# A four-layer model on one core: row statistics taken where the rows are finished, gates multiplied in at the expert slots, GpSimd joining a token's two expert rows, the input loaded in four pieces

## The reference

```python
def _layernorm(x, axis=-1, eps=1e-05):
    m = jnp.mean(x, axis=axis, keepdims=True)
    v = jnp.var(x, axis=axis, keepdims=True)
    return (x - m) / jnp.sqrt(v + eps)

for layer in range(4):
    xn = _layernorm(x)
    x = x + attn[layer](xn) + ffn[layer](xn)
```

```python
g = softmax(xn @ Wr)
top2_w, top2_idx = top_k(g, 2)
top2_w = top2_w / sum(top2_w)                 # layer 2 only
y = relu(xn @ W1[e]) @ W2[e]                  # for every expert e
out = sum(top2_w * y[top2_idx])
```

## Time and profile before

| what | value |
|---|---|
| time, median of 3 runs | 1793.24 us (1793.17 to 1802.02) |
| the profiled execution, its own time | 1782.04 us |
| its span | 1780.2 us |
| PE, PEld | busy 88%, 61% of the span |
| DVE, ACT, POOL | busy 66%, 56%, 21% |
| layer 0's second pair stage | from about 385 to 742 us of the span |
| norm stages of layers 1, 2, 3 | begin at 742.0, 1131.8, 1450.8 us |

### The profile page before, as it was taken

How to read it: one execution, slowest core, us unless ns; L and a number is a source line. 1 busy time by engine, 2 the same in 40 slices (tenths; PEclk the granted TensorE clock), 3 DMA queues, 4 the chain that set the end, 5 groups by cost and what they waited for, 6 DMA issues and landing times. The chain is left out here.

```text
span 1780.2 us, 31999 instructions
## 1 busy us (share of the span) xinstructions
PE 1575.2 (88%) x10960; PEld 1094.2 (61%) x10960; DVE 1183.5 (66%) x3106; ACT 1002.4 (56%) x2683; POOL 375.5 (21%) x386
## 2 busy tenths in 40 slices
PE   4799999959999999899999989588989957899986
PEld 2577777726666666567778766355556733555653
DVE  5599998747777777646545434577743358999964
ACT  2488887706666666444454434133453427888845
POOL 0100000000000000010122015332452410888830
PEclk8899999979999999989999999799999978999998
DMA  4000000040000000110000011400012130233200
GB/s 141 1 1 1 1 1 1 1 141 1 1 1 1 1 1 1 55 57 1 13 16 16 25 31 64 165 1 1 15 36 62 46 90 14 88 86 89 86 21 24
DMA packets 43980, 62.50 MB, mean 35 GB/s; under 512 B 7576, under 2 KB 29920, under 8 KB 43008
## 3 DMA queue, kind: packets, MB, share of 16 engines
q1 hardware_dynamic: 39280, 51.08, 9.6%
q0 software_dynamic: 4544, 9.38, 1.5%
HBM read 49.88 MB, written 15.75 MB: 37 GB/s over the span
## 5 line engine op out<-in xcount | busy, mean ns | idle before, releaser
L591 ACT ACTIVATE probs<-psum_all,pair_negmax 128x256 f32<-128x256 f32 x512 | 235.8, 473 | 158.9 <-DVE pair_negmax L690 86.7
L2116 POOL TENSOR_TENSOR weighted<-state,c_all 128x512 f32<-128x512 f32 x128 | 163.6, 1298 | 77.5 <-DVE state L2126 62.5
L690 DVE TENSOR_REDUCE pair_negmax<-psum_all 128x2 f32<-128x512 f32 x192 | 123.6, 685 | 66.9 <-PE psum_all L506 66.9
L2126 DVE TENSOR_TENSOR_SCAN state<-decay,psum_all 128x512 f32<-128x512 f32 x128 | 148.9, 1199 | 15.4 <-PE psum_all L2044 12.5
L716 DVE TENSOR_SCALAR probs<-probs,pair_recip 128x256 f32<-128x256 f32 x512 | 146.1, 349 | 4.5
L506 PE MATMUL psum_all<-keys,queryT 64*128 64x256 f32 x1024 | 143.9, 400 | 2.8 <-ACT probs L591 2.7
L602 ACT ACTIVATE probsT<-psum_all 128x512 f32<-128x512 f32 x256 | 140.0, 611 | 0.7 <-PE psum_all L517 0.5
L531 PE MATMUL psum_all<-probsT,values 128*64 128x256 f32 x1024 | 138.8, 392 | 0.0
L517 PE MATMUL psum_all<-ident,probs 128*128 128x128 f32 x1024 | 133.1, 273 | 2.8 <-ACT probsT L602 1.9
L517 PEld LDWEIGHTS psum_all<-ident,probs 128*128 128x128 f32 x1024 | 119.1, 141 | 18.1 <-issue 4.4
L506 PEld LDWEIGHTS psum_all<-keys,queryT 64*128 64x128 f32 x1024 | 92.6, 189 | 54.6 <-issue 46.6
(11 more groups left out here) (369 smaller groups left out, 3281.4 us busy)
## 6 DMA issues: line engine op xcount, KB each, us to landing
c_all<-c_rows SPq DMA_DIRECT2D x64, 256.0 KB, 3.3
slots<-slot_fill_dram SPq DMA_DIRECT2D x2, 2535.0 KB, 14.6
ring<-slots SPq DMA_DIRECT2D x18, 260.0 KB, 3.0
keys<-found SPq DMA_DIRECT2D x16, 256.0 KB, 4.7
up<-up_dram SPq DMA_DIRECT2D x1, 2048.0 KB, 7.8
down<-down_dram SPq DMA_DIRECT2D x1, 2048.0 KB, 12.3
up<-up_dram SPq DMA_DIRECT2D x1, 1408.0 KB, 6.1
found<-values,dest POOLq DMA_INDIRECT x78, 2.2
```

What stands on the lines that cost most here:

```text
L591: nc.scalar.activation(k.probs[:, 2 * (u % PAIR_BUF) + j, t, :], k.psum[score_bank(u, j)][:, SEQ * t:SEQ * (t + 1)], ACT.Exp, bias=k.pair_ ...
L690: nc.vector.reduce_max(k.pair_negmax[:, u % 2, SUB * j:SUB * (j + 1)], src, AXX, negate=True).then_inc(s.negmax_ready, 1)
L2116: nc.gpsimd.tensor_tensor(w.weighted[:, u % RING, :], w.state[:, u % RING, :], w.c_all[:, u // L3_DC % C_RING, :], ALU.mult)\
L2126: nc.vector.tensor_tensor_scan(w.state[:, u % RING, :], w.decay[:, u % L3_RING, :, :].rearrange("p b n -> p (b n)"), k.psum[u % PARTS_RING ...
```

## The change

It has six parts.

1. Statistics. A new `measure` issues `bn_stats` for some tiles, waits, and issues `bn_aggr` for them. `add_output` calls it for the two tiles of each sequence, `sparse_experts_stage` for each chunk of four tiles. `layer_norm_stage` then starts from the moments, except in layer 0.
2. The input is loaded by four transfers of 256 KB with a semaphore each, and `measure` runs on each when it has landed. TensorE waits for `ident` alone.
3. Gates travel with the rows: `gate_rows` copies the two gates behind each row, `SLOT_WIDTH` is 132, and layer 2's renormalising moves from step 20 to step 13.
4. In the expert stage three small VectorE instructions per chunk choose each slot's gate, ScalarE multiplies by it while it saves the result, and ScalarE and SyncE wait for the gates.
5. GpSimd adds the two rows of each token, one add of 128x512 for each chunk of four tiles. VectorE adds the sum to `k.x` by one add of 128x512, in place of eight instructions.
6. The expert stage has four more semaphores.

```diff
-SLOT_WIDTH = P + 2
+SLOT_WIDTH = P + 4
...
+def measure(nc, k, dve, step, tiles):
+
+    for t in tiles:
+        step.add(nc.vector.bn_stats(k.stats[:, t, :], k.x[:, t, :]))
+    step.wait()
+    for t in tiles:
+        step.add(nc.vector.bn_aggr(k.moments[:, t, :], k.stats[:, t, :]))
...
                 if first is not None:
-                    sp.dma_start(k.x[:, :, :], first).then_inc(s.x_loaded, 16)
+                    for c in range(CHUNKS):
+                        sp.dma_start(k.x[:, CT * c:CT * (c + 1), :], first[:, CT * c:CT * (c + 1), :]).then_inc(chunk_loaded[c], 16)
                     sp.dma_start(k.ident[:, :], k.dram["ident"]).then_inc(s.x_loaded, 16)
...
                 if first is not None:
-                    dve.wait_ge(s.x_loaded, 32)
-                for t in range(TILES):
-                    step.add(nc.vector.bn_stats(k.stats[:, t, :], k.x[:, t, :]))
-                step.wait()
-                for t in range(TILES):
-                    step.add(nc.vector.bn_aggr(k.moments[:, t, :], k.stats[:, t, :]))
-                step.wait()
+                    for c in range(CHUNKS):
+                        dve.wait_ge(chunk_loaded[c], 16)
+                        measure(nc, k, dve, step, range(CT * c, CT * (c + 1)))
+                    step.wait()
...
                 if first is not None:
-                    pe.wait_ge(s.x_loaded, 32)
+                    pe.wait_ge(s.x_loaded, 16)
                 keep_running(nc, k, 7, 5)
...
                     nc.vector.tensor_tensor(rows, k.mix[:, :, :], yb[:, 0:SEQ].rearrange("p (t n) -> p t n", t=SUB), ALU.add).then_inc(s.output_added, 1)
+                    dve.wait_ge(s.output_added, q + 1)
+                    measure(nc, k, dve, step, range(tile, tile + SUB))
...
+def gate_rows(nc, k, w, dve, s, step):
+
+    step.wait()
+    step.add(nc.vector.tensor_copy(w.rows[:, :, P + 2:P + 4].rearrange("p t r -> p r t"), k.gate_top[:, :, :]))
...
     if g == at.pick:
         gate_pick(nc, k, w, dve, s, step)
-    if g == at.renormalise and renormalise:
-        gate_renormalise(nc, k, w, dve, s, step)
+        if renormalise:
+            gate_renormalise(nc, k, w, dve, s, step)
+        gate_rows(nc, k, w, dve, s, step)
...
                     sp.wait_ge(s.dest_ready, c - CHUNK_RING + 1)
+                    sp.wait_ge(s.slots_gated, c - CHUNK_RING + 1)
...
-                        nc.scalar.activation(w.y_rows[:, j % 4, :], k.psum[6 + j % 2][:, 0:P], ACT.Copy).then_inc(s.y_saved, 1)
+                        act.wait_ge(s.slots_gated, j // SLOT_CHUNK + 1)
+                        nc.scalar.activation(w.y_rows[:, j % 4, :], k.psum[6 + j % 2][:, 0:P], ACT.Copy, scale=w.slot_gates[:, 2, j:j + 1])\
+                            .then_inc(s.y_saved, 1)
...
+                for c in range(CHUNKS):
+                    tiles = slice(CT * c, CT * (c + 1))
+                    pool.wait_ge(fetched[c], 32)
+                    nc.gpsimd.tensor_tensor(w.picked[:, 0, tiles, :], w.picked[:, 0, tiles, :], w.picked[:, 1, tiles, :], ALU.add).then_inc(s.joined, 1)
...
+                    gates = w.ring[:, c % CHUNK_RING, 0:count, P + 2:P + 4]
+                    nc.vector.scalar_tensor_tensor(w.slot_gates[:, 0, tiles], w.flags[:, tiles], 0.0, gates[:, :, 0], ALU.is_equal, ALU.mult)\
+                        .then_inc(s.halves_ready, 1)
+                    nc.vector.tensor_tensor(w.slot_gates[:, 1, tiles], w.flags[:, tiles], gates[:, :, 1], ALU.mult).then_inc(s.halves_ready, 1)
+                    dve.wait_ge(s.halves_ready, 2 * (c + 1))
+                    nc.vector.tensor_tensor(w.slot_gates[:, 2, tiles], w.slot_gates[:, 0, tiles], w.slot_gates[:, 1, tiles], ALU.add)\
+                        .then_inc(s.slots_gated, 1)
...
                 for c in range(CHUNKS):
-                    dve.wait_ge(fetched[c], 32)
-                    for r in range(2):
-                        for t in range(CT * c, CT * (c + 1)):
-                            if r == 1:
-                                dve.wait_ge(s.x_added, 2 * CT * c + t - CT * c + 1)
-                            nc.vector.scalar_tensor_tensor(k.x[:, t, :], w.picked[:, r, t, :], k.gate_top[:, r, t:t + 1], k.x[:, t, :], ALU.mult, ALU.add)\
-                                .then_inc(s.x_added, 1)
+                    rows = k.x[:, CT * c:CT * (c + 1), :]
+                    dve.wait_ge(s.joined, c + 1)
+                    nc.vector.tensor_tensor(rows, rows, w.picked[:, 0, CT * c:CT * (c + 1), :], ALU.add).then_inc(s.x_added, 1)
+                    dve.wait_ge(s.x_added, c + 1)
+                    measure(nc, k, dve, step, range(CT * c, CT * (c + 1)))
```

More of the change, by code:

```diff
@@ L2452, in use_experts_buffers @@
     values = k.values[:, :, :, :].rearrange("p i t n -> p (i t n)")
+    at = 3 * CHUNK + 2 * P + SLOT_TILES
+    w.slot_gates = flat[:, at:at + 3 * SLOT_TILES].rearrange("p (i n) -> p i n", i=3)
     w.hid_T = values[:, 0:2 * CHUNK].rearrange("p (i n) -> p i n", i=2)
```

12 lines of the change are left out of this document (7 added, 5 removed).

## The result

The changed kernel takes 1805.66 us (median of 7 runs, 1799.79 to 1808.09), the kernel before 1793.24 on the same chip: ratio 1.0063, 95% interval 1.0045 to 1.0082. Forecast were 1803.6 us, a ratio of 1.0058, and a range of 1796.5 to 1808. On another chip the ratio was later 1.0042 (1.0023 to 1.0061). So the change makes the kernel slower, by 0.4 to 0.6%.

A forecast was written before the change was run, and what follows sets the result against it. TensorE was taken as busy most of the span, VectorE counting only where another engine waits for it. Terms 5.3 + 0.55 + 4.0 + 0.4 + 0.1 = 10.35 us, added to 1793.24, gave 1803.6; range 1796.5 to 1808.

The forecast's parts named there:

- Pair stage (+5.3): Layer 0's second pair stage: nothing covers the statistics, 0.76 us at each of seven places, +5.3 us.
- The rival in which the stage takes them in: Second pair stage: VectorE's idle time absorbs the statistics, the 5.3 us vanish, 1798.3 us in total; chance 0.20.
- Layer 1's norm stage (+0.55): Stage before it ends 0.75 us later for the last sequence, norm stage gains 0.2; sum +0.55 us.
- the -0.2: Layer 1's norm stage: without statistics it gains only 0.2 us, since `keep_running` holds the first transposes.
- norm stages follow VectorE: Rival: dummy products give way, norm stages of layers 1 and 2 shorten by up to 4.4 us each; chance 0.06.
- Ends of the expert stages (+4.0): Layers 1 and 2: VectorE and GpSimd adds hold each other up, +2.0 us each; with the following norm stages +4.0.
- VectorE is the last: Ends of the expert stages: VectorE was taken as the last engine to finish, so its delay lengthens the stage.
- engines that don't hold each other up: Rival at the expert stages' ends: without mutual hold-up the tails cost 0.8 us each instead of 2.0; chance 0.16.
- Step 13 (+0.4): Layer 2's attention: renormalising and a copy delay the maxima 0.9 us, later idle time takes about half, +0.4 us.
- Expert loops (0): Expert loops: three small VectorE instructions and a wait per chunk, about 0.45 us, covered by idle time; 0.
- start (+0.1): First stage: a load ends it, three more transfer issues may delay the queue; +0.1 us, bounds 0 and 1.
- layer 3's stage (+0.2): Layer 3's norm stage: ends on a load; clearing four more semaphores delays SyncE's first load, +0.2 us.

The follow-up runs named there:

- experiment 12: Changed kernel with each sequence's statistics in the second pair stage taken one step later; ratio to the kernel before 1.0025, changed kernel 1.0042 on this chip.
- experiment 7: Changed kernel with the statistics of all rows taken at the head of the norm stages of layers 1, 2 and 3; ratio to the kernel before 1.0035.
- experiment 3: Changed kernel with a token's two rows added by VectorE instead of GpSimd at both expert stages' ends; ratio to the kernel before 1.0039.
- 8: Changed kernel with two VectorE adds per chunk, no GpSimd joins, statistics at the norm stages' heads, gates at step 15; ratio to the kernel before 0.9988.
- 11: As 8, with x loaded as one transfer; ratio to the kernel before 0.9986, median 1792.62 us against 1795.4.

## Why the prediction was right, and where it was not

- **Pair stage (+5.3).** Right: +5.4, seven steps of 0.77. The rival in which the stage takes them in fell here, but only for this place: one step later it does (experiment 12). The price was that of standing in front of `normalise` and of TensorE's next copy.
- **Layer 1's norm stage (+0.55).** The tail of the last sequence is +0.8, as forecast. The reading behind the -0.2, that `keep_running` and not VectorE holds the transposes back, was true of the profile in front by a hair: the products ended 6.23 us into the stage there and VectorE's first four tiles 6.29. In six of the eight profiles with statistics at this stage's head the products took only 4.53, and TensorE waited 1.8 us for VectorE. The rival "norm stages follow VectorE" was thus right in part in layer 1, though its gain was not the full 4.4: from start to logits the stage takes 12.4 to 15.4 us with the statistics and 13.1 to 13.6 without, 14.4 and 13.5 on average. In layer 2 it is 12.4 to 13.6 with them and 13.1 to 13.6 without, no gain.
- **Ends of the expert stages (+4.0).** The sum was right (+1.8 and +1.5 here; +1.85 and +2.0 between the first two profiles), but the mechanism holds only for layer 1's. There VectorE's third add is held up, 1.65 for an add of 0.69, and VectorE is the last engine, 0.55 us behind GpSimd. The rule of the Trainium skill (SBUF — State Buffer, "Who interferes with whom") agrees: GpSimd's third join, which began beside VectorE's add, took 1.6 instead of 1.26 by the same trade; both ended about 0.15 us sooner than a full wait and then the usual length would give. In layer 2's end the step that failed is "VectorE is the last". None of its adds is held up there in either profile of the changed kernel, and by itself it would have ended the stage 1.1 us sooner: 17.3 us of TensorE's idle time in place of 18.4, 0.9 over the first profile of before (and 0.4 over the one on the third chip), which is about the forecast's figure for engines that don't hold each other up. What makes +2.0 of it is GpSimd, which closes the stage 3.26 us behind its last instruction; no row in front showed me that, since nothing waited for it there. So that the second +2.0 came true was luck. Since VectorE's chain and GpSimd's end lie within 1.2 us of each other, taking the statistics away alone (experiment 7) saved nothing, GpSimd being last then at both ends; nor did it help to take GpSimd's joins away at the price of a second add per chunk on VectorE (experiment 3). Both together saved 3.2 to 4.0 us an end (8 and 11).
- **Step 13 (+0.4).** Mis-sized: 1.0 to 1.1. The idle time that was to take up half of it comes later in the step than TensorE's need for the bank.
- **Expert loops (0), start (+0.1), layer 3's stage (+0.2).** Layer 2's loop is 85.1 in all 14 profiles, although ScalarE's save with the gate takes 0.367 us instead of 0.278: that is covered. Layer 1's loop differs by more between profiles of one kernel (60.0 to 63.2) than a small cost would show. The first stage ends at 24.5 us on average with one transfer of `x` (24.2 to 24.9) and at 24.6 with four (23.6 to 25.3), so the +0.1 fits, and the +0.4 of the table says nothing against it, since it lies within what profiles of one kernel differ by. Layer 3's stage is 0.7 longer, mis-sized: SyncE's first load starts 0.27 later (2.02 instead of 1.75 into the stage), and the last takes 3.3 us to land instead of 2.9, which was not traced to a cause.
- **The total.** Forecast were +10.4 us; measured, +12.4 on the first chip and +7.6 on the third. That it lies so close is partly luck: step 13 and layer 3's stage cost 1.1 more than forecast, layer 1's norm stage 0.9 less on average where 0.2 was forecast, and the second expert stage's end has its +2.0 from another engine.
- **Reference.** Carrying the timed median over, instead of the profiled span, was what kept the forecast in place: the profile in front is 11 us faster than the chip's timed runs, and the experiments show that much between chips.

Not settled: why ScalarE's exponentials start 0.7 later at three steps on two of the chips, and what stops TensorE, ScalarE and VectorE for some 2 to 4 us once behind them.

## What to carry to other kernels

Work that is moved is paid for by what stands behind it at its new place, not by its length: look for the idle time of the engine in the timeline first, and put the work there, one step later if need be. Where a stage ends on several engines, look at each one's own end at the closing line, also of those for which nobody waits yet: if the change gives such an engine the last work, its end counts. Where two engines reach a point within 0.1 us of each other in one profile, that profile doesn't say which of them holds up the third; look at a second. Before two profiles are subtracted, profile both kernels on one chip.

## What was not expected of the hardware

- GpSimd ends an expert stage 3.24 to 3.27 us behind its last instruction in all 14 profiles, whether that is a join or the issue of a transfer. In the stages in which it sends rows to the slots it is 2.7 to 4.5, in the two with a long drain and no indirect transfer 0.07. That it is the indirect transfers that make it long was not tried alone.
- Two chips that run the same kernel before 12 to 14 us apart (1781.0 against 1793.2 and 1795.4) show part of it at fixed places of the program: three delays of about 0.7 us and one standstill of TensorE, ScalarE and VectorE in layer 2's attention. Each was used in one session of the experiments, so chip and session aren't told apart.
- With one dummy product in place of five the norm stages of layers 1 and 2 ran wholly at the lower of the two clock levels (granted clock 0.50), and lasted nearly as long (13.1 us to the logits, against 13.4 and 13.6).
- In layer 1's norm stage the five products ran at the full clock (4.53 us) in six of the eight profiles with statistics at its head and in none of the five without; what decides it was not tried.
